# A gated scan layer with a top-2 mixture of experts on one core: variances, slot tables, a norm sum and the last wait put elsewhere

## The reference, cut to what matters

```python
xn = _layernorm(x)                          # x: 8 sequences x 512 tokens x 256
g, v, d = xn @ Wg + bg, xn @ Wv + bv, xn @ Wd + bd
x_scan = sigmoid(g) * tanh(v)
a = 0.001 + 0.998 * sigmoid(d)
attn = scan(h[t] = a[t] * h[t-1] + x_scan[t])        # along the 512 tokens

scores = sigmoid(xf @ Wg.T + bg + bias)     # 8 experts, the two best of each token
h = gelu(einsum('td,ehd->teh', xf, W1) + b1)          # H = 1024
combined = einsum('ted,te->td', einsum('teh,edh->ted', h, W2) + b2, weights)
shared = gelu(xf @ Ws1.T + bs1) @ Ws2.T + bs2
out = x + attn + shared + combined
```

## Time and profile before

| | us |
|---|---|
| median of 3 runs | 710.67 (710.16 to 711.31) |
| the profiled execution | 710.67 |
| its span, first to last instruction | 708.8 |
| PE busy | 665.5 (94%) |
| DVE busy | 513.5 (72%) |
| ACT busy | 430.4 (61%) |
| POOL busy | 285.4 (40%) |

### The profile page before, as it was taken

How to read it: one execution, slowest core, us unless ns; L and a number is a source line. 1 busy time by engine, 2 the same in 40 slices (tenths; PEclk the granted TensorE clock), 3 DMA queues, 4 the chain that set the end, 5 groups by cost and what they waited for, 6 DMA issues and landing times.

```text
span 708.8 us, 20193 instructions
## 1 busy us (share of the span) xinstructions
PE 665.5 (94%) x5872; PEld 521.3 (74%) x5873; DVE 513.5 (72%) x1329; ACT 430.4 (61%) x738; POOL 285.4 (40%) x261
## 2 busy tenths in 40 slices
PE   4879999999999999699999999999999999999993
PEld 3455747565656565488988888888888888898773
DVE  5878989898989888766667666676666666666652
ACT  7967776868686855455555555555555555555651
POOL 2132332323242424234554645545446455463421
PEclk9999999999999999999999999999999999999997
DMA  7424334342516131222433323334333243332421
GB/s 258 169 71 139 90 120 112 97 137 71 172 57 182 35 120 31 70 44 60 67 52 61 67 53 66 57 60 66 55 60 66 53 67 54 61 65 50 72 40 23
DMA packets 54172, 57.55 MB, mean 81 GB/s; under 512 B 13204, under 2 KB 48916, under 8 KB 54136
## 3 DMA queue, kind: packets, MB, share of 16 engines
q1 hardware_dynamic: 38456, 38.42, 18.4%
q0 software_dynamic: 15680, 18.69, 16.4%
HBM read 38.53 MB, written 18.55 MB: 81 GB/s over the span
## 4 chain that ended last, share of the span: by engine, by line
PE 75%; DVE 13%; issue 5%; ACT 3%; DMA 2%; POOL 0%; DVEq 0%; SPq 0%; ACTq 0%; POOLq 0%
PE bank L1213 33%; PE bank L1205 29%; PE bank L1232 3%; PE bank L1193 3%; PE bank L1262 2%; PE bank L1244 2%; DVE W L800 2%; DVE arena L896 1%; DVE arena L839 1%; DVE arena L897 1%; PE bank L1184 1%; DVE arena L852 1%; DVE small L809 1%; DMA arena<-in_gates 1%; PE bank L1149 1%
## 5 line engine op out<-in xcount | busy, mean ns | idle before, releaser
L1213 PE MATMUL bank<-W,arena 128*128 (+1 forms) x2304 | 305.8, 274 | 16.0 <-DVE arena L897 14.0
L1205 PE MATMUL bank<-rows,W 128*128 128x256 f16 (+1 forms) x1920 | 299.2, 294 | 0.3 <-issue 0.2
L1213 PEld LDWEIGHTS bank<-W,arena 128*128 128x128 f16 x2304 | 222.4, 98 | 58.0 <-DVE arena L897 20.4
L1205 PEld LDWEIGHTS bank<-rows,W 128*128 (+1 forms) x1920 | 186.2, 98 | 54.5 <-issue 0.8
L592 ACT ACTIVATE arena<-bank,par 128x256 f32<-128x256 f32 x256 | 134.0, 559 | 80.3 <-PE bank L1205 69.3
L502 POOL DMA_INDIRECT out<-arena,slot_add x64 | 109.7, 1714 | 146.4 <-ACT arena L729 136.6
L896 DVE TENSOR_SCALAR arena<-arena,par 128x256 f16<-128x256 f32 x284 | 101.7, 358 | 81.7 <-ACT arena L592 54.8
L897 DVE SCALAR_TENSOR_TENSOR arena<-arena,par 128x256 f16<-128x256 f32 x284 | 138.7, 488 | 10.1
L438 POOL DMA_INDIRECT lists<-entry,place x64 | 67.9, 1061 | 150.6 <-ACT arena L578 73.2
L487 POOL DMA_INDIRECT rows<-xhl_rows,slot_list x64 | 68.9, 1076 | 51.8 <-DMA slot_list<-lists 34.8
L600 ACT ACTIVATE rows<-bank 128x1024 f16<-128x1024 f16 x32 | 32.7, 1023 | 60.9 <-PE bank L1262 33.4
(11 more groups left out here) (157 smaller groups left out, 519.9 us busy)
## 6 DMA issues: line engine op xcount, KB each, us to landing
stage<-in_w SPq DMA_DIRECT2D x32, 512.0 KB
b2row<-in_b SPq DMA_DIRECT2D x39, 128.0 KB
arena<-in_x SPq DMA_DIRECT2D x8, 512.0 KB
xhl_rows<-W SPq DMA_DIRECT2D x8, 512.0 KB
out<-arena SPq DMA_DIRECT2D x8, 512.0 KB
W<-in_w SPq DMA_DIRECT2D x4, 512.0 KB, 9.3
lists<-entry,place POOLq DMA_INDIRECT x64
rows<-xhl_rows,slot_list POOLq DMA_INDIRECT x64
```

What stands on the lines that cost most here:

```text
L1205: ins = T.matmul(bank_, weights(w, wp * HALF + c * H + j * P, P), rhs[:, 2 * xp + c, :], start=n == 0, stop=n == 3 * KD - 1)
L1213: ins = T.matmul(banks[t // 2][:, (t % 2) * D:(t % 2 + 1) * D], h[:, hp, t * P:(t + 1) * P], weights(w, (2 + wp) * HALF + j * D, D), start ...
```

## The change

It has six parts.

1. In sequences 1 to 6 `variances(b + 1)` moves from before `scan_input(b, 0)` to behind `scan_input(b, 1)`.
2. In sequence 7 the two shared results of sequence 6 move behind the first scan.
3. The slot tables come in pieces. What the first 31 slots need (`FIXED`) stays in sequence 7, in two parts behind splits 1 and 2, and sets `route_ok` to 1. The rest, for the last 8 slots, becomes `late_tables`, seven pieces of 3 or 4 small instructions (23 in all, on up to 64 columns) between the splits of slots 0 and 1, and sets it to 2. SP waits for 2 before slot 24, PE before slot 30. DVE writes slots 0, 1 and 2 out before its loop. `SPREAD` of sequence 7 changes with it.
4. In sequence 0 PE does the norm sum behind group 2 in place of 4; DVE does the scales behind the second residual and `x_low` behind split 5.
5. In the last small slot `result` of the slot before moves from behind the third to behind the second split.
6. SP in place of POOL waits for the last adds.

```diff
-SPREAD = {None: (10, 11, 13, 14, 16, 18, 20), SEQS - 2: (9, 10, 11, 12, 13, 14, 15), SEQS - 1: (4, 5, 6, 7, 8, 9, 10)}
+SPREAD = {None: (10, 11, 13, 14, 16, 18, 20), SEQS - 2: (9, 10, 11, 12, 13, 14, 15), SEQS - 1: (5, 6, 7, 8, 9, 9, 10)}
+FIXED = BIG - 1
...
         @block.sync
...
+            sp.wait_ge(route_ok, 2)
             for n in range(BIG - 8, BIG):
...
             sp.wait_ge(o_out, 16 * SEQS)
+            for u in range(2):
+                sp.wait_ge(add_out[u], BIG * 16 + 16 * ((SMALL + 1 - u) // 2))
...
         @block.gpsimd
...
-            for u in range(2):
-                pool.wait_ge(add_out[u], BIG * 16 + 16 * ((SMALL + 1 - u) // 2))
...
             def opening():
...
                 residual(0, 0, 1)
+                scales(1)
                 split_wide(0, 4)
-                scales(1)
+                split_wide(0, 5)
                 x_low(1)
-                split_wide(0, 5)
                 low_part(1, 0, 0)
...
             def sequence(b, u, last_=False):
...
                 if last_:
                     places(b, u)
-                shared_result(b - 1, 0)
-                shared_result(b - 1, 1)
-                if not last_:
+                else:
+                    shared_result(b - 1, 0)
+                    shared_result(b - 1, 1)
                     for part in range(5):
                         best_two(b, part)
-                    variances(b + 1, 1 - u)
                 scan_input(b, 0)
                 scan(b, 0)
+                if last_:
+                    shared_result(b - 1, 0)
+                    shared_result(b - 1, 1)
                 scan_input(b, 1)
+                if not last_:
+                    variances(b + 1, 1 - u)
...
-                    if last_ and i in (1, 2, 4):
-                        tables((1, 2, 4).index(i))
+                    if last_ and i in (1, 2):
+                        tables(i - 1)
...
             def tables(part):
                 if part == 0:
                     own.settle()
                     seq(V.tensor_tensor(count, carry, ebase, ALU.subtract))
...
                     seq(V.tensor_copy(twos, twos_i))
                     own.mark(V.tensor_tensor_scan(pad_end, one, twos, 0.0, ALU.mult, ALU.add))
+                    own.mark(V.tensor_scalar(room, twos, -1.0, float(TOKENS), ALU.mult, ALU.add))
+                    return
+                own.settle()
+                full = [P, FIXED, E]
+                seq(V.tensor_tensor(ended, pad_end.unsqueeze(1).to_broadcast(full),
+                                    starts[:, 0:FIXED].unsqueeze(2).to_broadcast(full), ALU.is_le))
+                own.mark(V.tensor_tensor(moved, ended, room.unsqueeze(1).to_broadcast(full), ALU.mult))
+                own.mark(V.tensor_reduce(sets[:, 0:FIXED], ended, AX.X, ALU.add))
+                own.settle()
+                own.mark(V.tensor_reduce(addr[:, 0:FIXED], moved, AX.X, ALU.add))
+                own.mark(V.tensor_scalar(slot_set[:, 0:FIXED], sets[:, 0:FIXED], float(E - 1), 1.0, ALU.min, ALU.add))
+                own.settle()
+                V.tensor_tensor(slot_at[:, 0:FIXED], addr[:, 0:FIXED], starts[:, 0:FIXED], ALU.add).then_inc(route_ok, 1)
+                dve.wait_ge(route_ok, 1)
+
+            def late_tables(part):
...
+                if part == 0:
+                    seq(V.tensor_copy(pad, pad_i))
+                    seq(V.tensor_tensor(odd, pad, twos, ALU.subtract))
+                    seq(V.tensor_tensor_scan(odd_end, one, odd, 0.0, ALU.mult, ALU.add))
...
+                    V.tensor_tensor(slot_at[:, tail], addr[:, tail], odd_addr, ALU.add).then_inc(route_ok, 1)
+                    dve.wait_ge(route_ok, 2)
...
-            def slot(n, u, first=False):
+            def slot(n, u, first=False, late=()):
                 for j in range(KH):
                     split_h(n * KH + EV_A + j, n * KH + H_A + j, j, par[u][:, :], first)
                     if j == 0 and not first:
                         result(n - 1, 1 - u)
+                    if j in late:
+                        late_tables(late[j])
...
-                    if k == 2:
+                    if k == (2 if n + 1 < SLOTS else 1):
                         result(n - 1, 1 - u)
...
-            slot(0, 0, first=True)
-            with own.loop(BIG // 2 - 1, 2 * KH) as it:
+            slot(0, 0, first=True, late={1: 0, 2: 1, 4: 2, 5: 3})
+            slot(1, 1, late={2: 4, 4: 5, 6: 6})
+            slot(2, 0)
+            with own.loop(BIG // 2 - 2, 2 * KH) as it:
                 for v in range(2):
-                    slot(it * 2 + 1 + v, (1 + v) % 2)
+                    slot(it * 2 + 3 + v, (1 + v) % 2)
...
         @block.tensor
...
-                    if i == (4 if first else 2 if last_ else 0):
+                    if i == (2 if first or last_ else 0):
                         pe.wait_ge(place_ok, b + 1)
                         norm_sum(b + 1, ps_l[:, 128:130])
...
+            pe.wait_ge(route_ok, 2)
             w = slot(BIG - 2, 0, weight_set(BIG - 2))
```

More of the change, by code:

```diff
@@ L218, in layer @@
         sets = rt[:, 420:420 + SLOTS]
-        ended = arena[:, 2048:2048 + SLOTS * E].rearrange("p (i e) -> p i e", e=E)
-        moved = arena[:, 2560:2560 + SLOTS * E].rearrange("p (i e) -> p i e", e=E)
-        odd_ended = arena[:, 2880:2880 + E * E].rearrange("p (i e) -> p i e", e=E)
-        odd_moved = arena[:, 2944:2944 + E * E].rearrange("p (i e) -> p i e", e=E)
+        ended = arena[:, 2048:2048 + FIXED * E].rearrange("p (i e) -> p i e", e=E)
+        moved = arena[:, 2560:2560 + FIXED * E].rearrange("p (i e) -> p i e", e=E)
+        late_ended, late_moved, odd_ended, odd_moved = (
+            rt[:, i * E * E:(i + 1) * E * E].rearrange("p (i e) -> p i e", e=E) for i in range(4))
         bank = [ctx.enter_context(nc.psum_tensor(f"bank{i}", [P, 512], F32)) for i in range(8)]
@@ L966, in sequence @@
                         scan(b, 1)
-                    if i == 1 and not last_:
-                        scales(b + 1)
-                    if i == 3 and last_:
+                    if i == (3 if last_ else 1):
                         scales(b + 1)
```

56 lines of the change are left out of this document (27 added, 29 removed).

## The result

The changed kernel takes 689.15 us (median of 4 runs, 688.91 to 689.43) against 710.94 for the kernel before beside it: a ratio of 0.9695, 95% interval 0.9678 to 0.9712. That is 2.25 us above the forecast of 686.9, inside its range. The profiled execution took 689.23 with a span of 687.4, which is 21.4 less than before.

A forecast was written before the change was run, and what follows sets the result against it. PE was taken as the bound, so only its idle or low-clock time or the end after its last matmul counts. Terms -3.6 - 8.8 - 8.4 + 0 - 0.7 - 2.3 = -23.8 took 710.67 to 686.9 us; range 685.0 to 693.5.

The forecast's parts named there:

- opening: Sequence 0: the 3.65 us wait and 1.7 of low clock go, new waits cost 1.7; -3.6 us, bounds -1.5 to -5.
- sequences 1 to 6: Scan ends 2.0 us earlier, PE stops waiting; -8.8 us from sequences 2 to 6, sequence 1 gains nothing; bounds -5.0, -9.1.
- sequence 7 and switch: Idle PE of 8.8 us and 1.8 of clock shrink by all but the waits left; -8.4 us, bounds -5 and -10.
- late tables: Slots 0 and 1: 23 small instructions, 4.6 us, fit in DVE's 8.0 us left; 0, or +1 if a split came late.
- result(37) earlier: Last small slot: result(37) starts 0.75 us earlier and the last adds follow; -0.7 us, 0 to -0.8.
- SP in place of POOL: Kernel end: POOL's 4.22 us DRAIN begins at about 702.1 and the add lands under it; -2.3 us, 0 to -2.4.
- rival A: Kernel end: POOL's DRAIN ends only some 4.2 us after the last landing, SP saves nothing; 689.2 us, 25%.
- The step named as the tightest: Sequences 2 to 6: of 4.9 us between POOL's norm shift and ACT's normed rows, 0.4 us is left.
- 0.5 in small ones: Switch: 0.5 us of small waits left, beside about 1.0 before group 6 and 0.6 before the rows.
- B: Sequences 2 to 6: variances only change places, split 0 waits for them; 4.8 of 8.8 us kept, 690.9, 15%.
- rival C: Switch: scatters or splits 2 us later, PE stands about 2.5 us, clock halved once more; 690.6 us, 15%.
- Rival D: Slots: DVE's loop wrap makes each slot's first split late, PE loses it in 28 slots; at 1 us 715, 2%.

The follow-up runs named there:

- the variances alone: The kernel before with the next sequence's variances moved behind the second scan input: 702.81 us against 711.30, ratio 0.9882.
- the loads' edit: The changed kernel with PE's two register loads of slot_set at the switch taken out of the path: 688.33 us, ratio 0.9678 to the kernel before.
- the switch alone: The kernel before with tables in pieces, late tables, shared results behind the first scan and new SP and PE waits: 705.99 us against 711.30, ratio 0.9924.
- the doubled statistics: The changed kernel with the variances' four statistics instructions done twice in sequences 1 to 6: 697.66 us, ratio 0.9813 to the kernel before.
- the one with GpSimd waiting: The changed kernel with the wait for the last adds given back to GpSimd: 692.48 us, ratio 0.9732 to the kernel before.
- SP's order on it: The kernel before with SP reading both addresses first, issuing both list loads, then reading slot_set: 711.66 us against 711.17, ratio 1.0008.
- the opening alone: The kernel before with norm sum behind group 2, scales ahead of split 4, x_low behind split 5: 708.24 us against 711.30, ratio 0.9958.
- the end alone: The kernel before with result(37) ahead of the last slot's third split and SP waiting for the adds: 708.48 us against 711.30, ratio 0.9960.

## Why the prediction was right, and where it was off

| term | predicted | measured in the profiled executions |
|---|---|---|
| opening | -3.6 | -3.49 (55.42 to 51.93) |
| sequences 1 to 6 | -8.8 | -8.58 (199.55 to 190.97) |
| sequence 7 and switch | -8.4 | -6.29 (45.77 to 39.48) |
| late tables | 0 | 0 (344.20 both) |
| result(37) earlier | -0.7 | -0.62 (issue of the last add; the result itself -0.75) |
| SP in place of POOL | -2.3 | -2.43 (8.44 to 6.01) |
| sum | -23.8 | -21.4 (span 21.4) |

The forecast of 686.9 was 2.25 us too low, and nearly all of that is one term. The measured 689.15 is just what rival A named (689.2), and that is chance: the runs above refute its mechanism.

**Opening.** Right, and by its own steps: the new waits were put at 1.0 and 0.7 us and are 0.84 and 0.45, and the clock does not fall behind them.

**Sequences 2 to 6.** Right. The chain of steps (scan earlier, gelu 0 earlier, split 0 behind the variances, PE no longer waiting) is in the trace, and the variances alone give 8.5 us. The doubtful point was that some 0.7 us above the floor stood in waits too short for the list. They are there: in sequence 3 of before, group 0 starts 1.26 us later behind the logits than in the changed kernel, for a listed 1.10, and group 1 is 1.70 later, so another 0.44 us with no wait listed. The first sequence kept its 31.7 us, as forecast. The step named as the tightest, POOL's shift and ACT's normed rows, held: ACT came to the normed rows at 130.01 without a wait.

**Sequence 7 and the switch: the mis-sized term.** The mechanism was right: SP's wait for the address is gone, and its wait for the lists is the later one. The address comes 21.5 us after the logits (264.4), as forecast (276.6 - 254.97 = 21.6). Off was the size, 2.1 us, in two steps.

First, 0.6 us: the sum had the rows 7.5 us earlier, because the lists would be as early as before. PE's row transposes come 6.9 us earlier, 32.72 us after the logits in place of 39.63. The last scatter indeed starts 20.16 us after the logits, before 20.20. But it landed later. Before, SP had the lists at 285.29 - 7.5 = 277.8, 2.6 us after a scatter issued at 275.17. After, the scatter and SP's first read of slot_at, which follows the lists at once (timeline, then the instructions of L350 with first and last start):

```profile
263.06 1.07 POOL L442 DMA_INDIRECT lists<-entry,place  x1 [0.30 <-ACT arena L586]
```

```profile
L350 SPq TENSOR_LOAD <-slot_at x3: 273/273/472, 266.4 to 279.6; - x3
```

That is 3.3 us. From the issue to the end of SP's wait it is 3.1 to 4.0 us in six traces with the new tables, and 2.5 to 2.9 in five with the old ones. PE's wait for rows is 1.60 us here, not the forecast 0.6, and not under the 1.2 that was named as the sign (0.6 by the later rows, 0.4 since PE itself came earlier), and 2.3 to 2.7 in four of those six traces. Why a scatter lands later here is open.

Second, 1.5 us: "0.5 in small ones" stood for all that lies behind the rows, and two register loads of 2.02 us were there. They couldn't be read as a wait in the trace of before, since the array ran at a low clock there and its sequencer had time. The fault of the step is that it took away the low clock and asked of every engine what is late next, but not of PE's own sequencer. The runs show 1.8 to 2.1 us for these loads in the changed kernel at the full clock, of which some 0.6 go with SP's load beside the second. At the low clock of the kernel before they show 0.1, by one pair of traces.

**Late tables, tail.** Right, term by term. The result of slot 37 comes 0.75 us earlier, but the add behind it took 3.79 us to land in place of 3.66, so the last issue gained 0.62. Rival A (25%) and B (15%) fall by the runs. Of rival C the condition came true in part: lists late, PE idle 4.7 us at the switch; the low clock that it also needs came behind the rows in three traces of other kernels with the new tables (the loads' edit, the switch alone, the doubled statistics) and not in the changed kernel's two. Rival D: the slots take 344.20 us in both, the wrap costs nothing.

**The parts and the whole.** Alone the four parts give 8.5 + 3.1 + 5.3 + 2.8 = 19.7 us, together 21.8. Of the 2.1 between, 0.4 is sequence 1 behind the opening and 0.9 the switch, whose clock fell in one case only. The rest, 0.8 us, is open; it is no more than the medians of the kernel before and its own executions (710.16 to 712.54) leave in doubt. Inside the opening (norm sum, scales, x_low) and inside the switch (shared results, tables) no run took one edit alone, so how their gains divide is not shown.

## What to carry to other kernels

Where a stretch runs at a low clock behind a long wait, other costs can be hidden under it: before booking the wait and the clock as gained, read what the sequencer of that engine does there (register loads, loop entries), and price it at the full clock. When a stall is taken away, order the issuing engine's register reads so that only those of the next transfer stand between its semaphore and its issue. And put the last wait of a kernel on an engine whose DRAIN is short, so that the long one runs beside the landing.

## What the runs showed of the hardware

- **GpSimd's DRAIN behind indirect transfers:** 4224 ns from its start with the transfer landed, begun 2.3 to 2.5 us after the end of the last issue (the kernel before and the one with GpSimd waiting). Begun beside the issue it took 6005 ns and ended 4.23 us after the end of that issue; the transfer was still under way for the first 2.3 us of these. SP's took 7 ns in the same place, ACT's 837, PE's 570, DVE's 522. The Trainium skill (VectorE: DVE Perf Modes, section "The DRAIN you can't avoid") gives about 12 ns for all five; of these SP alone is near it.
- **A register load is not one price:** 273 to 472 ns on SP in L350; 323 and 489 ns on PE; 858 to 889 ns for SP's load of slot 2's weight set, with or without a load of PE beside it; 928 to 958 ns for PE's where it overlaps that one. The Trainium skill (DMA: Bandwidth & Descriptors, section "Latency and other measured facts") puts its floor at about 600 ns; most rows here are under that.
- **The length of a wait alone does not decide the clock:** behind waits for rows of 2.32, 2.51, 2.71 and 4.09 us the next 12 matmuls took 2.31 to 2.77 us, behind waits of 2.46 (the kernel with GpSimd waiting) and 3.57 us they took 1.47. In kernels with the old order of sequence 7, a wait of 2.10 us stands before group 5: the 12 matmuls behind it took 1.48 us in the kernel before, but 1.83 and 1.92 with SP's order on it and in the opening alone; in the end alone they took 1.50, and the next 12, behind a wait of 0.88, 2.74. Waits of 0.85 and 1.60 us left the clock at 1.00 in both traces of the changed kernel.
- **A wait costs PE some 0.16 us more than its row says** (1.01 for 0.85, 1.26 for 1.10, 0.48 for 0.30). Matmuls in a row show the same 0.16: group 1 of sequence 0 starts at 34.89 and its row lasts 1.47, and what follows starts at 36.20.
